# Attention and graph layers on one core: results kept in their PSUM banks, key products in two halves of the inner index, half of the Strassen weights loaded between them

## What is computed

```python
h = maximum(layernorm(x), 0)                       # layer 0: attention
weight = adj * exp(query(h) @ keyt(h).T)
x = x + (weight / weight.sum(axis=2)) @ value(h)
h = maximum(layernorm(x), 0)                       # layer 1: graph convolution
agg = adj @ h / maximum(adj.sum(-1), 1e-6)
x = x + relu(concatenate([h, agg], axis=2) @ W.T)
```

## Time and profile before

| | |
|---|---|
| median of 3 runs | 1933.32 us (1931.07 to 1945.87) |
| the profiled execution's own time | 1942.48 us |
| its span | 1940.4 us |
| TensorE busy | 1892.7 us, 98% |
| VectorE, GpSimd, ScalarE busy | 81%, 57%, 44% |
| DMA engines busy, moved | 57%, 370.5 MB |

### The profile page before, as it was taken

The page is one execution under the profiler, slowest core; times in us unless marked ns, Lnnn a source line. Parts: engine busy times, 40 slices in busy tenths (PEclk is TensorE's granted clock), DMA queues, the critical chain, the costliest instruction groups (busy, mean ns, idle before and its releaser), DMA issues.

```text
span 1940.4 us, 29261 instructions
## 1 busy us (share of the span) xinstructions
PE 1892.7 (98%) x8956; PEld 1576.8 (81%) x8956; DVE 1579.6 (81%) x2649; ACT 862.4 (44%) x1453; POOL 1103.0 (57%) x1066
## 2 busy tenths in 40 slices
PE   8899999999999999999999999999999999999997
PEld 5778888888888888888788888888888888887885
DVE  6887888888788888888878888887888878888776
ACT  4344444444444445443445443444444454434442
POOL 4665565565565565655655655655655656546552
PEclk9999999999999999999999999999999999999999
DMA  6456656566656566555566555566555665555632
GB/s 222 148 189 212 210 181 196 188 203 207 210 178 190 198 205 204 192 198 173 189 208 219 188 194 184 191 211 211 179 191 194 204 203 194 197 173 184 211 125 87
DMA packets 190881, 370.69 MB, mean 191 GB/s; under 512 B 17936, under 2 KB 115216, under 8 KB 182672
## 3 DMA queue, kind: packets, MB, share of 16 engines
q1 hardware_dynamic: 190864, 370.48, 57.2%
HBM read 266.60 MB, written 103.81 MB: 191 GB/s over the span
## 4 chain that ended last, share of the span: by engine, by line
PE 49%; DVE 19%; DMA 17%; issue 8%; SPq 4%; POOL 2%; ACT 1%; DVEq 1%; POOLq 0%; ACTq 0%
PE bank L518 16%; PE bank L520 16%; PE bank L519 16%; DMA turned_store<-blocks 8%; DMA n_l<-t_store 8%; DVE y L1223 3%; SPq L263 3%; DVE x L1235 3%; DVE stats L1091 2%; DVE x L1227 2%; DVE g_full L1213 2%; DVE deg L1112 1%; DVE mean_sum L1096 1%; DVE blocks L1073 1%; DVE sums L1252 1%
## 5 line engine op out<-in xcount | busy, mean ns | idle before, releaser
L403 POOL TENSOR_TENSOR hT_l<-turned,hT_h 128x512 fp32r<-128x512 f32 x122 | 181.9, 1517 | 264.0 <-ACT hT_h L824 263.9
L242 POOL TENSOR_TENSOR w_l<-w,w_h 128x512 fp32r<-128x512 f32 x62 | 80.3, 1295 | 307.5 <-ACT w_h L857 307.5
L1073 DVE STREAM_TRANSPOSE blocks<-h 128x512 f32<-128x512 f32 x252 | 163.3, 685 | 110.3 <-DMA turned_store<-blocks 110.3
L518 PE MATMUL bank<-hT_h,n_h 128*128 128x512 f32 x512 | 200.9, 392 | 3.9 <-DVE hT_l L1164 2.8
L519 PE MATMUL bank<-hT_l,n_h 128*128 128x512 f32 x512 | 200.2, 391 | 0.0
L520 PE MATMUL bank<-hT_h,n_l 128*128 128x512 f32 x512 | 200.2, 391 | 0.0
L518 PE MATMUL bank<-wv_h,hT_h 128*128 128x512 f32 x512 | 199.6, 390 | 0.0
L519 PE MATMUL bank<-wv_l,hT_h 128*128 128x512 f32 x512 | 199.5, 390 | 0.0
L520 PE MATMUL bank<-wv_h,hT_l 128*128 128x512 f32 x512 | 199.3, 389 | 0.0
L399 POOL TENSOR_TENSOR xb<-x_in,bv_b 128x512 f32<-128x512 f32 x128 | 165.9, 1301 | 43.5 <-DVE x L1235 39.3
L843 ACT ACTIVATE kz_h<-bank,kp_bias 128x512 fp32r<-128x512 f32 x128 | 83.6, 675 | 207.5 <-PE bank L520 207.5
(11 more groups left out here) (152 smaller groups left out, 5394.9 us busy)
## 6 DMA issues: line engine op xcount, KB each, us to landing
turned_store<-blocks SPq DMA_DIRECT2D x126, 512.0 KB, 4.5
turned<-turned_store SPq DMA_DIRECT2D x504, 128.0 KB, 2.9
x_in<-x SPq DMA_DIRECT2D x32, 1024.0 KB, 5.3
n_h<-t_store SPq DMA_DIRECT2D x31, 1024.0 KB, 6.3
n_l<-t_store SPq DMA_DIRECT2D x31, 1024.0 KB, 8.3
out<-x SPq DMA_DIRECT2D x124, 256.0 KB, 2.0
n_h<-n_store SPq DMA_DIRECT2D x60, 512.0 KB, 4.6
n_l<-n_store SPq DMA_DIRECT2D x60, 512.0 KB, 5.9
```

What stands on the lines that cost most here:

```text
L242: engine.tensor_tensor(w_l[:, g], w[:, g], w_h[:, g].bitcast(F32), ALU.subtract).then_inc(w_split, 1)
L403: pool.tensor_tensor(by_blocks(hT_l, t), turned_tile(t), by_blocks(hT_h, t).bitcast(F32), ALU.subtract).then_inc(hT_split, 1)
L518: pe.matmul(dst, lh, rh, start=first, stop=False, skip_group_check=more)
L1073: nc.vector.transpose(blocks[:, :, :, t % NT, :].rearrange("p j c b -> p c j b"), h[:, t, :].rearrange("p (c j b) -> p c j b", c=DT, b=Q)) ...
```

## The change

The arithmetic, the number of instructions of each kind and the bytes moved stay. What moves:

- **PSUM in place of SBUF.** `exp` writes over the scores in their bank, and `weigh` reads it there; `v` of tiles 2 and 3, which write banks 0 and 1, wait for `weigh` in place of `exp`. `sum_z` adds in the Y bank. The layer's result is written over the az product in its bank. TensorE's waits for `y_done` become waits for `x2_done`. `exp` no longer waits for `degrees`, and both graphs' `exp` stand together.
- **Key products in halves.** All four outputs take inner tiles 0 and 1, then all four take 2 and 3. After the first half `load_t(0)` loads T1 (1 MB) into the freed half, ahead of the load of x; T2 follows at the old place.
- **Order.** VectorE's `degrees` and the first `turn_g` come ahead of the low key parts. In the first step W1 is loaded earlier, n is stored later, and mixes and splits change places. In the final step z comes ahead of A22, S4 and `degrees`.

```diff
-            def load_t(i):
-                sp.wait_ge(kp_psum, DT * (i + 1))
-                sp.dma_start(n_h[:, :, :].bitcast(F32), t_d[0]).then_inc(t_loaded, 16)
-                sp.dma_start(n_l[:, :, :].bitcast(F32), t_d[1]).then_inc(t_loaded, 16)
+            def load_t(k):
+                half = slice(2 * k, 2 * k + 2)
+                sp.dma_start(n_h[:, half, :].bitcast(F32), t_d[0, :, half, :]).then_inc(t_loaded[k], 16)
+                sp.dma_start(n_l[:, half, :].bitcast(F32), t_d[1, :, half, :]).then_inc(t_loaded[k], 16)
...
             def step(i):
                 j = i - 1
+                if is_first(i):
+                    sp.wait_ge(n_stored, 32)
+                    sp.wait_ge(t_stored, 64)
+                sp.wait_ge(kp_half, i + 1)
+                load_t(0)
                 sp.wait_ge(xb_done, T * (i + 1))
                 load_x(i + 1)
                 move_g(j)
-                load_t(i)
+                sp.wait_ge(kp_psum, DT * (i + 1))
+                load_t(1)
...
             def all_kp(i):
                 pe.wait_ge(hT_split, T * i)
                 if not is_first(i):
-                    pe.wait_ge(n_loaded, 64 * (i - 1))
-                kp(i, 0)
-                kp(i, 1)
+                    pe.wait_ge(n_loaded[0], 32 * (i - 1))
+                kp(i, 0, 0)
+                kp(i, 1, 0)
                 if not is_first(i):
-                    pe.wait_ge(y_done, T * (i - 1))
-                kp(i, 2)
+                    pe.wait_ge(x2_done, T * (i - 1))
+                kp(i, 2, 0)
                 pe.wait_ge(sum_inv_done, i)
-                kp(i, 3)
+                kp(i, 3, 0)
+                if not is_first(i):
+                    pe.wait_ge(n_loaded[1], 32 * (i - 1))
+                for dt in range(DT):
+                    kp(i, dt, 1)
...
             def v(i, t):
                 if t >= 2:
-                    pe.wait_ge(exp_done, NT * (G * i + t - 1))
+                    pe.wait_ge(w_done, G * i + t - 1)
...
-                nc.vector.tensor_tensor(z_sum[r], bank[Y_BANK[r]][:, :], z_sum[r], ALU.add).then_inc(z_summed, 1)
+                nc.vector.tensor_tensor(bank[Y_BANK[r]][:, :], bank[Y_BANK[r]][:, :], p0_copy[r], ALU.add).then_inc(z_summed, 1)
...
-                nc.vector.scalar_tensor_tensor(out=place[:, t, :], in0=y[:, :], scalar=0.0, in1=place[:, t, :],
+                nc.vector.scalar_tensor_tensor(out=place[:, t, :], in0=bank[az_bank][:, :], scalar=0.0, in1=place[:, t, :],
```

More of the change, by code:

```diff
@@ L504, in final_step @@
                 low_part(j, A12)
-                for m in (S1, S3, S2, A22):
+                for m in (S1, S3, S2):
                     low_part(j, m)
                 low_at(j)
+                low_part(j, A22)
                 low_part(j, S4)
@@ L552, in _, with kp @@
             pe.wait_ge(n_split, DT)
-            def kp(i, dt):
+            def kp(i, dt, half):
                 cols = slice(dt * P, (dt + 1) * P)
-                product(bank[KP_BANK[dt]][:, :],
-                        [(n_h[:, c, cols], n_l[:, c, cols], hT_h[:, c, :], hT_l[:, c, :]) for c in range(DT)]
-                        ).then_inc(kp_psum, 1)
+                mm = product(bank[KP_BANK[dt]][:, :],
+                             [(n_h[:, c, cols], n_l[:, c, cols], hT_h[:, c, :], hT_l[:, c, :])
+                              for c in range(2 * half, 2 * half + 2)], start=half == 0, stop=half == 1)
+                if half == 1:
+                    mm.then_inc(kp_psum, 1)
+                elif dt == DT - 1:
+                    mm.then_inc(kp_half, 1)
             def first_kp():
@@ L563, in first_kp @@
                 for dt in range(DT):
-                    kp(0, dt)
+                    for half in range(2):
+                        kp(0, dt, half)
             def all_kp(i):
@@ L775, in final_step @@
                 pe.wait_ge(part_split, 7 * j + S1)
-                pe.wait_ge(y_done, T * j - 1)
+                pe.wait_ge(x2_done, T * j - 1)
                 strassen(j, 2, 0)
-                pe.wait_ge(y_done, T * j)
+                pe.wait_ge(x2_done, T * j)
                 strassen(j, 2, 1)
@@ L880, in high_z @@
                 if g == 0:
-                    high(kz_h[:, t, :], z_sum[r], z_summed, ROUNDS * j + r + 1, z_high)
+                    high(kz_h[:, t, :], bank[Y_BANK[r]][:, :], z_summed, ROUNDS * j + r + 1, z_high)
                 else:
@@ L932, in layer0 @@
                 relu_norm(1, src, j, 1)
+                high_kp(i, 0)
                 high_kp(i, 1)
@@ L952, in layer0 @@
                 high_part(j, A12)
-                exp(i, 1)
                 high_w(i, 1)
@@ L1307, in layer0 @@
                 turn_g(j, 0)
-                low_kp(i, 2)
-                low_kp(i, 3)
+                for dt in range(DT):
+                    low_kp(i, dt)
                 turn_g(j, 1)
```

135 lines of the change are left out of this document (65 added, 70 removed).

## The result

| | before | after |
|---|---|---|
| median of 4 runs each, same chip | 1933.05 us | 1905.65 us (1905.35 to 1905.90) |
| ratio, with its 95% interval | | 0.984 (0.9816 to 0.9863) |
| the profiled execution's own time | 1942.48 us | 1905.82 us |
| its span | 1940.4 us | 1904.0 us |

A forecast was written before the change was run, and what follows sets the result against it. TensorE was taken to bound the kernel, losing 27.3 us over 29 periods against its 57.96 us floor. Steady part 24.4, start 8 and end 6 make 38.4 off the profiled 1942.5: 1904 us, range 1897 to 1918.

The forecast's parts named there:

- Part 1: Periods: with key products halved and T1 loaded early, the whole wait for T1's load goes; 27.3 us lost there.
- Part 2: Periods: PSUM for SBUF frees 2.6 us of VectorE each, none on TensorE's path; layer 0's statistics end 1.5-2 us earlier.
- The steady part: The 29 periods: 27.3 us of loss goes, 2.9 us stays, so -24.4 us.
- S2 late next: Periods: S2's low part, without slack, is the next thing late; by engine sequence some 0.5 us earlier than before.
- residual of 0.1 a period: Periods: wait still left for S2's low part, 2.9 us in all; bounds nothing or 0.5 us per period.
- Rival B: Periods: GpSimd's serial chain from w_h replaces the wait, S2 0.4 us late each; 1916 us, chance 11%.
- Rival C: Periods: second weigh, behind x's statistics, holds v of tile 3 on TensorE; slower, 1953 us, chance 3%.
- The start: First step: reordered loads, mixes and splits shorten the gaps for hT_l, low key parts and T1; -8 us, bounds 0 and -12.
- lower clock behind the gaps: First step: time lost to low clock after the hT_l and low-key-part gaps is regained, -3.1 us.
- Rival A: First step: reordering only moves its gaps and gives nothing; 1912 us, chance 20%.
- The end: Final step: 4.7 us wait for second low z and 1.7 us of low clock go; taken as -6, bounds -3 and -7.
- Rival D: Key products: eight bank changes in place of four drop TensorE's clock, 10.9 us per period; 2220 us, chance 1%.

The follow-up runs named there:

- banks alone: Kernel before with exponentials, z and the layer's result in PSUM banks, orders and loads unchanged: 1914.25 us, ratio 0.9861.
- halves alone: Kernel before with the key products in two halves and T1 loaded early between them, nothing else: 1920.95 us, ratio 0.9893.
- exp apart: Kernel after with the second graph's exponentials put back behind the high part of A12: 1904.17 us, ratio 0.9812.
- T1 late: Kernel after with both halves of the t load at the old place, behind both moves of g: 1905.10 us, ratio 0.9812.
- after again: Kernel after, unchanged, timed and profiled once more: 1906.82 us, ratio 0.9836 to the kernel before.
- old final step: Kernel after with the final step's order of before (z behind A22, S4 and degrees): 1913.32 us, ratio 0.9827.
- order of layer 0: Kernel before with only degrees, first transpose and ScalarE's first two relu_norm moved ahead of key parts: 1958.69 us, ratio 1.0093.

## Why the prediction was right, and where its reasons were not

- **The floor and the base.** That TensorE sets the pace, that 57.96 us is its floor and that 27.3 us were to be had over 29 periods, all held: 27.25 came. So did the choice to subtract from the profiled 1942.5 and not from the median of 1933. That the wait is what varied fits the times (the kernel before took 1931 to 1946 us, the kernel after 1905.35 to 1905.90), but there is one profile of the kernel before, so it is not shown.
- **The step that failed** is the attribution. "So the whole of this wait goes" was true of Part 1 by itself, but "none of it on TensorE's path today" was false of Part 2. The prediction named the very chain (statistics, transpose, both moves, n_l) and the 1.5 to 2 us that the banks would give it, and did not carry them on to the issue of t at 11.42, where 0.3 us was lacking at the median. The banks alone take 26.8 of the 27.25 us, and the early T1 adds nothing to them. The steady part came out right all the same because the floor caps both.
- **The sum was partly luck.** The four stretches missed their forecasts by +4.4, -2.9, +1.8 and -1.4 us, which add up to only 2.0.
- **S2 late next.** It was put 0.5 us earlier as a sequence and came 0.7 earlier (its end 22.05 to 21.34 from the scores, medians), against a need of 22.10. The residual of 0.1 a period, 2.9 us in all, was not there. With the halves alone S2 ended at 21.81, and 3.7 us were left over the 29 periods, but not as forecast: 1.4 of them stand in the first, where TensorE waits 1.2 for S2's low part, and the rest is scattered. w_h was put 0.2 to 0.4 later and came 0.29 later (its end 7.03 to 7.32). Rival B's chain does not hang on it: S2's low part ends at 21.3 in every kernel with the result in its bank, whether the first w_h starts at 4.7 (banks alone), 5.0 (exp apart) or 6.7 (after).
- **Rival C** had the second `weigh` too late: it ends at 7.49 in place of 10.69, with 11.2 wanted. The early T1 hardly delayed x: it lands 5.8 us after its issue at the median, and 5.7 with T1 late.
- **The start** was mis-sized: -8 forecast, -3.6 measured. The profile shown above is not the usual case: the distance before the key products of pair 1 (the wait for hT_l) did not fall in it, and the one for the low key parts went wholly:

```profile
70.88 0.50 PE L525 MATMUL bank<-hT_h,n_h 128*128 128x512 f32 x1 [2.97 <-DVE hT_l L1177]
...
109.33 0.50 PE L525 MATMUL bank<-n_h,hT_h 128*128 128x512 f32 x1 [0.85 <-POOL hT_l L415]
```

  In the four other profiles with the same first step (after again, T1 late, exp apart, old final step) the two distances are 1.7 to 1.8 and 1.6 us, against 3.17 and 3.95 before, and the start is as long. The terms of the forecast, beside the kernel after, again (us; distances between starts of matmuls):

| term | forecast | measured |
|---|---|---|
| first sum | 0 | +2.07 |
| hT_l | -1.9 | -1.45 |
| low key parts | -2.1 | -2.33 |
| T1 | -1.5 | -0.53 |
| lower clock behind the gaps (measured: all the rest) | -3.1 | -1.35 |

  So the two gaps were sized well, and the clock, T1 and the first sum were not. The first sum comes 1.8 to 2.1 later (61.74 and 61.97 against 59.90): GpSimd's mixes, moved up, now lie beside VectorE's split of w and stretch it, and it is at 59.38 with the old first step and at 59.06 with one mix moved behind. The forecast had moved them without that cost. Rival A, that the start gives nothing, fell too.
- **The end** was undersized: -7.4 for -6. It was reckoned that S2 would be 0.9 late; TensorE's only wait in the final step is one of 0.3.
- **The last step** had no term: +1.8, for a wait that the periods hide. The later w_h of Part 1 was priced in the periods only, where it has slack.
- **Rival D**, the clock: all 29 periods are at the floor, at a granted clock of 1.00, so the eight bank changes of the key products cost nothing. The Trainium skill ("TensorE: Matmul & The Clock Gate", A second HAM failure mode: psum-queue depth-cycling) warns of an oscillation when groups cycle through banks; no run here shows one.

## What to carry to other kernels

When a wait names a DMA, follow its issue back through the queue to the compute engine that releases it: shortening an instruction there by 0.45 us, four times, did what moving the transfer did, and doing both paid once. Ask first how much is lacking: here it was 0.3 us at the median. A gain that can't exceed the distance to a floor should be forecast from the floor, and each part priced alone as well as together, since a reorder that is free behind other edits (order of layer 0) cost 0.9% without them. Price an edit also in the first and last step, where the work that hides it is missing.

## What the hardware showed

- VectorE instructions with both inputs in SBUF stretch beside GpSimd, some of them by far more than the mean tells. The addition of the positive part took 692 ns where GpSimd is idle and 1143 as the mean in the periods; with one input in a bank it stayed at 692 in the same periods. The subtraction of w_h took 2.32 us (3.4 times the 0.68 of the same line behind it) beside long additions of GpSimd, and the sum over half a tile 2.50 in place of 0.42. The two ended 0.55 and 0.27 us behind the GpSimd instruction beside them, as if each had waited for it; two cases do not show it as a rule. The Trainium skill ("GPSIMD Engine Reference", Specifications) has the shared interface; the size of the effect is from these rows.
- The exponentials in their bank cost ScalarE no more: 438 ns against 465 for a write to SBUF, both on 128 x 256.
- How long the loads of t took to land varied with their size and with what was in flight beside them. From the issue of n_l, medians of periods 3 to 29: 8.3 us for the 2 MB of before in two loads, 6.1 for T2's 1 MB at the same place of the queue, 5.2 for T1's 1 MB ahead of x, and 7.2 and 8.7 where both were issued one behind the other (after, T1 late).
